# Pre-norm layer, 1 core: ScalarE copies the turned rows of maxima, Pool makes the low half of six transposed tiles

## The reference

```python
x = x + attention(layernorm(x))      # softmax(q k^T / 4 + alibi + causal) v, then Wo, bo
x = x + ffn(layernorm(x))            # quantised w1, w2, w3
# ffn: hidden = sigmoid(x @ w1q.T) * (x @ w2q.T);  out = hidden @ w3q.T
```

## Time and profile before

| | |
|---|---|
| median of 3 runs | 620.85 us (620.85 to 621.74) |
| the profiled execution | 619.34 us, of which 617.6 us are the span from the first to the last instruction |
| PE busy | 584.6 us |
| DVE busy | 462.5 us |
| ACT busy | 364.4 us |
| POOL busy | 183.4 us |
| mean granted TensorE clock | 0.994 |

### The profile page before, as it was taken

How to read it: one execution, slowest core, us unless ns; L and a number is a source line. 1 busy time by engine, 2 the same in 40 slices (tenths; PEclk the granted TensorE clock), 3 DMA queues, 4 the chain that set the end, 5 groups by cost and what they waited for, 6 DMA issues and landing times.

```text
span 617.6 us, 10828 instructions
## 1 busy us (share of the span) xinstructions
PE 584.6 (95%) x3448; PEld 364.1 (59%) x3448; DVE 462.5 (75%) x1204; ACT 364.4 (59%) x781; POOL 183.4 (30%) x394
## 2 busy tenths in 40 slices
PE   7889889999999999999999999999999999999997
PEld 5565456565657565555556565555455556566487
DVE  5878998677878876578787878788888888812187
ACT  3456457665654547567475456576676576587721
POOL 7646422361342241340212422203200220252510
PEclk9999899999999999999999999999999999999999
DMA  7995743752313116423131131146141130011001
GB/s 201 276 279 161 192 123 91 205 164 64 88 37 105 37 39 195 143 78 88 38 93 30 38 105 35 53 128 170 37 123 36 38 89 1 0 47 46 2 18 34
DMA packets 27452, 57.50 MB, mean 93 GB/s; under 512 B 5316, under 2 KB 14916, under 8 KB 23940
## 3 DMA queue, kind: packets, MB, share of 16 engines
q1 hardware_dynamic: 27156, 56.43, 32.6%
q10 hardware_dynamic: 240, 0.39, 0.3%
HBM read 40.69 MB, written 14.80 MB: 90 GB/s over the span
## 4 chain that ended last, share of the span: by engine, by line
PE 76%; DVE 15%; issue 4%; ACT 2%; POOL 1%; DMA 1%; ACTq 0%; POOLq 0%; DVEq 0%
PE pO L1182 19%; PE pS L1163 19%; PE pM L1143 17%; DVE pm L1352 5%; PE pM L1118 5%; DVE pM L1355 3%; PE pM L1051 3%; PE pM L1126 3%; PE pM L1104 2%; PE pM L1059 2%; PE pS L1118 1%; PE pS L1051 1%; PE pM L1163 1%; ACT probs L955 1%; DVE st L1240 1%
## 5 line engine op out<-in xcount | busy, mean ns | idle before, releaser
L955 ACT ACTIVATE probs<-pS 128x512 f32<-128x512 f32 (+3 forms) x610 | 288.9, 548 | 159.3 <-PE pS L1163 157.1
L1352 DVE TENSOR_REDUCE pm<-pM 128x1 f32<-128x512 f32 x384 | 239.0, 680 | 42.8 <-PE pM L1143 42.1
L1143 PE MATMUL pM<-kst,qst 126*128 126x512 f32 (+3 forms) x640 | 228.1, 386 | 10.3 <-DVE pm L1355 3.8
L1163 PE MATMUL pS<-qst,kst 128*128 128x512 f32 (+3 forms) x610 | 234.1, 401 | 3.6 <-ACT probs L955 2.2
L1163 PEld LDWEIGHTS pS<-qst,kst 128*128 128x128 f32 x610 | 114.0, 190 | 82.5 <-issue 43.4
L1143 PEld LDWEIGHTS pM<-kst,qst 126*128 126x128 f32 x640 | 120.2, 191 | 50.6 <-DVE pm L1352 14.7
L1355 DVE CUSTOM_DVE_ANT_0 pM<-pM,mask 128x128 f32<-128x128 f32 (+3 forms) x256 | 118.7, 517 | 38.8 <-PE pM L1143 38.5
L831 POOL TENSOR_SCALAR_AFFINE_SELECT probs<-probs 128x128 f32<-128x128 f32 x256 | 75.6, 308 | 217.5 <-ACT probs L955 210.0
L1182 PE MATMUL pO<-probs,vals 128*17 128x512 f32 (+3 forms) x1264 | 133.5, 537 | 0.0
L1182 PEld LDWEIGHTS pO<-probs,vals 128*17 128x17 f32 x1264 | 29.9, 97 | 65.1 <-issue 38.8
L1118 PE MATMUL pM<-x2T,wT 128*128 128x256 f32 x264 | 39.0, 288 | 1.4 <-DVE pm L1355 0.7
(11 more groups left out here) (161 smaller groups left out, 402.8 us busy)
## 6 DMA issues: line engine op xcount, KB each, us to landing
kst<-parts SPq DMA_DIRECT2D x78, 256.0 KB
qst<-parts SPq DMA_DIRECT2D x30, 256.0 KB, 4.0
parts<-qk_hl SPq DMA_DIRECT2D x28, 256.0 KB, 4.3
ctx_dram<-ctx_raw SPq DMA_DIRECT2D x15, 256.0 KB, 3.6
xin<-in_L_attn_x SPq DMA_DIRECT2D x5, 512.0 KB, 4.8
out<-work SPq DMA_DIRECT2D x8, 256.0 KB, 4.2
work<-ctx_dram SPq DMA_DIRECT2D x7, 256.0 KB
work<-rden_dram SPq DMA_DIRECT2D x7, 256.0 KB
```

What stands on the lines that cost most here:

```text
L955: nc.scalar.activation(probs[:, n % PSLOTS, q0:CH], score(n)[:, q0:CH], ACT.Exp)\
L1143: pe.matmul(max_bank(x)[:, 0:N], qst[0:R_MAX, u % QSLOTS, h, t * P:(t + 1) * P], kst[0:R_MAX, n % KSLOTS, h, 0:N], start=True, stop=True). ...
L1163: pe.matmul(score(n)[:, q0:CH], kst[0:R_END, sl, h, b:b + P], qst[0:R_END, u % QSLOTS, h, q0:CH], start=True, stop=True).then_inc(scores_r ...
L1352: nc.vector.tensor_reduce(dst, bank, AX.X, ALU.max).then_inc(max_free, 1)
```

## The change

The copy of the turned rows to `mT` goes from VectorE (`split_max`) to ScalarE (`copy_max`), after the exponential and the side group of the same place in the order; for unit 1 the swap is moved from after h = 0 to after h = 1 of step 2. For the six `x2T` groups of the loop ScalarE writes a second, unrounded copy `x2T_f` in SBUF ahead of the high part, and Pool, which works on SBUF, subtracts the high part from it. The bank of such a group, and the `up` that reads it, then wait for Pool (`side_p`).

```diff
-    swap_in = {(first_step[1] - 2, 0) if u == 1 else at: u for at, u in swap_in.items()}
+    swap_in = {(first_step[1] - 2, 1) if u == 1 else at: u for at, u in swap_in.items()}
...
-        return "v" if g in head_splits else READS_LAST[g[0]]
+        return "v" if g in head_splits else "p" if g in by_pool else READS_LAST[g[0]]
...
+    by_pool = [g for g in side if g and g[0] == "x2T"]
...
-            eng.wait_ge(side_a if e == "a" else side_v, n)
+            eng.wait_ge({"a": side_a, "v": side_v, "p": side_p}[e], n)
...
+            def split_x2(g):
+                pool.wait_ge(half_a, half_no[g] + 1)
+                nc.gpsimd.tensor_tensor(x2T_of(g)[:, 1, :, :], x2T_f[:, :, :], x2T_of(g)[:, 0, :, :].bitcast(F32),
+                                        ALU.subtract).then_inc(side_p, 1)
+                need_empty(pool, g)
...
                 if g and g[0] in "kq":
                     split_lo(g)
+                if g and g[0] == "x2T":
+                    split_x2(g)
...
-                    nc.scalar.activation(x2T_of(g)[:, 0, :, :], bank(g).rearrange("p (k n) -> p k n", k=KT), ACT.Copy)\
-                        .then_inc(half_a, 1)
+                    src = bank(g).rearrange("p (k n) -> p k n", k=KT)
+                    if g in by_pool:
+                        if by_pool.index(g):
+                            need_empty(act, by_pool[by_pool.index(g) - 1])
+                        nc.scalar.activation(x2T_f[:, :, :], src, ACT.Copy)
+                    nc.scalar.activation(x2T_of(g)[:, 0, :, :], src, ACT.Copy).then_inc(half_a, 1)
...
+            def copy_max(u):
+                x = ("swap", u)
+                act.wait_ge(max_ready, ready_to[use_no[x] + 1])
+                if u >= 1:
+                    act.wait_ge(m_in, 16 * u)
+                nc.scalar.activation(mT[:, :], max_bank(x)[0:2 * G * TPC, 0:P], ACT.Copy).then_inc(mT_ok, 1)
...
-            for g in (V01, *XT, K10, Q10):
+            for g in (V01, *XT, K10):
                 side_op(g)
+            copy_max(0)
+            side_op(Q10)
...
                     if h == SIDE_AFTER and side[s]:
                         side_op(side[s])
+                    if swap_after(s, h):
+                        copy_max(swap_after(s, h))
...
-                elif kind == "x2T":
+                elif kind == "x2T" and g not in by_pool:
...
-            def split_max(u):
-                x = ("swap", u)
-                dve.wait_ge(max_ready, ready_to[use_no[x] + 1])
-                if u >= 1:
-                    dve.wait_ge(m_in, 16 * u)
-                nc.vector.tensor_copy(mT[:, :], max_bank(x)[0:2 * G * TPC, 0:P]).then_inc(mT_ok, 1)
...
-            split_max(0)
...
-                    if swap_after(s, h):
-                        split_max(swap_after(s, h))
```

More of the change, by code:

```diff
@@ L307, in preln_layer @@
         mask = sb("mask", [P, CH], BF16)
+        x2T_f = sb("x2T_f", [P, KT, HALF])
         ident = sb("ident", [P, P])
@@ L399, in preln_layer @@
         side_v = sem("side_v")
+        side_p = sem("side_p")
         half_a = sem("half_a")
```

## The result

The changed kernel takes 630.74 us (median of 4 runs, 629.34 to 631.40), the kernel before 621.12 us. The ratio is 1.0158, 95% interval 1.0132 to 1.0184: 1.6% slower, 9.6 us. The forecast was 628.0 us, range 624.5 to 631.5; its likeliest case alone had the range 626.5 to 629.5, which the measurement is above.

The account below looks back on a forecast made before the run. TensorE's order was taken to bound the kernel. Five new waits for Pool, 7.55 us, less a gain of 0.4 made 7.15 us; on the runs' median of 620.85 us that gave 628.0 us, range 624.5 to 631.5.

Parts of the forecast that it names:

- likeliest case: Whole kernel: the forecast itself, 628.0 us, own range 626.5 to 629.5, stalls 0.3 us longer or shorter each; chance 0.53.
- TensorE's order bounds the time: Whole kernel: TensorE busy 584.6 of 617.6 us; another engine counts only where TensorE stands still for it.
- The gain: TensorE's waits for VectorE: removing 8.5 us of VectorE's work wins back 0.4 us, bounds 0 and 1.5.
- term of 0.27 us in step 10: Behind unit 2's copy: VectorE has no pause until TensorE's 1.51 us wait in step 10, so 0.27 us come back.
- moved swap: Unit 1's swap in step 2: next exponentials start at about the same time; taken as 0, bounds 0.3 us either way.
- The five stalls: TensorE waits for Pool's subtraction of the x2T groups of steps 31, 38, 75, 82 and 142; 7.55 us in sum.
- Pool's price: Pool's new subtraction: median 1.28 us, as L838, once 2.22, against VectorE's 0.69.
- the rival of five slow subtractions: At the five stalls: every subtraction takes the slow 2.22 us, adding 4.7 us, sum 12.2; no chance of its own given.
- Other signs: At the mT copies: no TensorE wait for `qst<-mT`; `mT` copied within 0.3 us of each swap of units 5 and later.
- The second copy: ScalarE's extra x2T copy, 0.61 us: delays all behind it by 0.5 to 0.6 us.
- The clock falls in a stall: After the new stalls of 1.7 and 2.25 us: one or two clock falls give 629.7 to 631.4 us; chance 0.2.
- my own sign against it: TensorE, whole execution: the prediction is wrong if TensorE is busy longer in sum, meaning a clock matter; no size given.

Follow-up runs that it names:

- spaced: early_split with one more step between each first x2T group of a chunk and its first up; 621.35 us, ratio 1.0018 to the kernel before.
- two_copies: The changed kernel, but VectorE subtracts from the bank as before; ScalarE keeps both x2T copies and the maxima copy; 621.06 us, ratio 1.0008 to the kernel before.
- bank_by_act: The changed kernel, but the next user of an x2T bank waits only for ScalarE's second copy; 623.93 us, ratio 1.0054 to the kernel before.
- early_split: bank_by_act with Pool subtracting after clear_future of h = 1 on diagonal steps, ahead of h = 2 and 3; 621.27 us, ratio 1.0006 to the kernel before.
- max_only: Kernel before plus only ScalarE's copy of the maxima and unit 1's moved swap; VectorE keeps all x2T subtractions; 618.58 us, ratio 0.9960.
- before_again: The kernel before, unchanged, run once more for its profile; 621.58 us.
- max_again: max_only repeated unchanged against the kernel before; 619.56 us, ratio 0.9987.
- max_h0: max_only with the swap of unit 1 back after h = 0 of step 2; 619.99 us, ratio 1.0001 to the kernel before.
- warm: The changed kernel with 18 unread transposes ahead of up's wait for Pool in step 143; 630.04 us, ratio 1.0148 to the kernel before.

## Why the prediction was right, and what it missed

*TensorE's order bounds the time.* Right. VectorE lost 22 instructions, and TensorE's waits of turns for it went from 6.4 to 6.2 us; spaced against two_copies shows no worth of the lighter VectorE even with Pool out of the way. The gain was put at 0.4 us; at step 15 the profile shows 0.1. Its term of 0.27 us in step 10 did not come: that wait is 1.51 us in both kernels. What is there comes in part from the moved swap, put at 0: step 3 gained 0.25 us. VectorE's busy time fell by 6.5 us, not 8.5, as neighbouring instructions overlap: in the trace of before the 16 copies of 0.27 us cover only 2.4 us in which VectorE does nothing else.

*The five stalls.* Right in place and size, and in cause in four of the five. Predicted 1.05, 1.7, 0.9, 1.65 and 2.25 us, sum 7.55. The shifts of TensorE's steps were 1.14, 1.75, 0.82, 1.75 and about 2.2 (3.8 less 1.6 for the clock; 2.27 in bank_by_act, whose clock did not fall there), sum 7.7. bank_by_act shows the bank as the cause of those in steps 39 and 83, early_split Pool's place behind the clearings as cause of half of the one in step 143. In step 76 I had the bank too, but without it 0.65 us of the 0.82 stay; two_copies puts 0.49 us there on the second copy. That wait for Pool was 0.42 us, below the 0.9 that I gave as the least.

*Pool's price.* It took 1.26 to 1.30 us each time, as the median row had it. The one slow row of 2.22 us has a cause that the trace of before shows:

```profile
64.24 2.22 POOL L838 TENSOR_TENSOR qk_hl<-qk_f,qk_hl 128x512 fp32r<-128x512 f32 x1
...
64.31 1.00 DVE L1388 SCALAR_TENSOR_TENSOR work<-vals,thr,work 128x768 bf16<-128x768 f32 x1
```

In all 13 profiles this subtraction runs beside this VectorE instruction for 0.90 to 1.00 us, and takes 2.04 to 2.22 us. None of the other subtractions of this kind runs beside it, nor do the six new ones, and all of them take 1.26 to 1.30 us. It can go the other way: at 122.33 of before VectorE's L1365, 0.17 us with no work of Pool beside it, started 0.21 us after such a subtraction and took 1.09 us, while Pool kept its 1.26 us. The Trainium skill, SBUF — State Buffer, Who interferes with whom, says that a VectorE instruction with two SBUF inputs contends with GpSimd's reads; the trace agrees. So the rival of five slow subtractions was rightly left out.

*Other signs.* No wait for `qst<-mT` is left. `mT` was copied within 0.1 us of its swap in nine of the eleven units from 5 on; in units 5 and 15 it took 0.53 and 0.74 us, more than the 0.3 that I gave.

*The second copy.* I priced it inside the stalls, and did not say that it costs by itself. two_copies shows 0.5 us in each of three steps, 1.5 us, with no subtraction on Pool at all. In the changed kernel it is inside the five stalls and not on top of them, since in each TensorE goes on only when Pool is done.

*The terms that were off: the clock, and a rest.* I gave "The clock falls in a stall" 0.2 and kept it out of the sum. What came is nearer to this rival (629.7 to 631.4 us) than to my likeliest case, and my own sign against it, TensorE busy longer in sum, is there with 5.4 us. The range held because it took the clock in. The profiled execution has two such stretches more than that of before, 1.58 us and about 1.6, which with 7.7 us of stalls and 0.7 for the late transfer, less 0.1 gained, makes 11.5 us of the 11.4 measured. Only one of the two stands behind a new stall. The other is in step 44, where before has it too in some executions; that it came in this one is chance, and no part of my reasoning.

In medians the loss is 9.6 us, 2.5 more than the sum. Three of the four executions of the changed kernel have a mean granted clock of 0.988 or 0.989, median 630.73 us; the 13 of before at this clock have 621.86. At the same clock the loss is thus 8.9 us, and the clock is 0.7 us of the 2.5. This is an estimate from few executions; if the typical execution of before has one stretch less, the price of a stretch makes it up to 1.6. The stalls less the gain measured 7.6 us where I had 7.15, which is another 0.4. The 0.4 to 1.3 us that are left stay open; the late transfer of 0.7 us is seen in one execution, and no run tells how often it comes.

## What to carry to other kernels

Before work moves to a slower engine, list everything that waits for its end. Here it was the next reader and, four uses on, the next user of the PSUM bank, although the new engine did not read that bank; a release that is named after the last writer of the result holds the buffer too long. An in-order engine starts moved work behind what stands ahead of it in its program: place it by when its input comes. Taking work off an engine that already waits for the bounding one bought nothing here; what max_only gained, about 1 us, came from a moved swap and a wait that went.

## What the runs showed of the hardware

The granted clock of TensorE fell to 0.5, 1.2 instead of 2.4 GHz, at places that changed between executions of the same instructions. Step 44 has three pauses for VectorE, 0.19, 0.49 and 0.66 us, within 3 us, and they are the same to 0.01 us in all 13 profiles. The stretch of 0.5 behind them is in the profiles of before_again (214.7), max_again (215.3), max_h0 (213.4), warm (216.6) and the changed kernel (217.5), and not in the other eight, before and max_only among them. Here is before's profile, whose clock stayed at 1.00 with TensorE busy 2.14 of 3.42 us:

```profile
210.33:213.75 3.42, 2.14 (x9) 1.10 (x7) 3.30 (x16) 1.98 (x5) 1.67 (x4) 1.00 0.59 154
```

In step 44 such a stretch cost 1.51 to 1.59 us. In 12 executions of one kernel the times spread from 616.2 us, at a mean granted clock of 0.999, to 621.7 us at 0.989 (max_again). So differences under 0.4% between these kernels need many executions, and a single profile can be 3 us away from another of the same kernel.
